# Normalising the last group's attention outputs token by token, and issuing the tail's regrouping transfers from two engines

## The reference

```python
x = x + _L0_conv_ref(_gn(x), w_qkv, w_o)      # attention: 12 heads of 16, 1024 tokens
x = x + _L1_conv_ref(_gn(x), w1, b1, w2, b2, bias_w, bias_b)
# _L0: attn = softmax(q k^T * 16 ** -0.5);  out = (attn @ v) @ w_o
# _L1: rfftn over the 32 x 32 positions, two block matmuls (4 blocks of 48) with
#      bias and relu on the complex spectrum, irfftn; plus x @ bias_w.T + bias_b
```

## Time and profile before

| | |
|---|---|
| median of 3 runs | 1517.59 us (1516.69 to 1521.7) |
| profiled execution, its time | 1528.75 us |
| profiled execution, its span | 1527.0 us |
| TensorE, busy | 1445.3 us (95%) |
| VectorE, busy | 1158.3 us (76%) |
| ScalarE, busy | 1009.0 us (66%) |
| GpSimd, busy | 187.6 us (12%) |
| queue q1 (all of the kernel's transfers) | 100992 packets, 105.44 MB, 30.1% of 16 engines' span |
| chain that ended last | PE 80%, DVE 6%, DMA 6%, SPq 2% |

### The profile page before, as it was taken

The page is one execution under the profiler, slowest core; times in us unless marked ns, Lnnn a source line. Parts: engine busy times, 40 slices in busy tenths (PEclk is TensorE's granted clock), DMA queues, the critical chain, the costliest instruction groups (busy, mean ns, idle before and its releaser), DMA issues.

```text
span 1527.0 us, 27399 instructions
## 1 busy us (share of the span) xinstructions
PE 1445.3 (95%) x9972; PEld 695.3 (46%) x9972; DVE 1158.3 (76%) x2153; ACT 1009.0 (66%) x2017; POOL 187.6 (12%) x277
## 2 busy tenths in 40 slices
PE   7699989999999999999999999999999999999787
PEld 4344333444545454444545444544544443434354
DVE  3695888888789878987789878997799878874131
ACT  1064777577767777677767777677767777668312
POOL 2000000140001300140011300040012100030000
PEclk7696999999999999999999999999999999999988
DMA  4430312213332414323422324333431333211313
GB/s 113 73 64 2 84 29 61 62 56 81 80 92 64 87 45 103 78 68 76 92 85 58 82 69 85 71 83 65 89 85 43 78 91 77 66 35 50 77 28 80
DMA packets 101126, 107.19 MB, mean 70 GB/s; under 512 B 25152, under 2 KB 77824, under 8 KB 100992
## 3 DMA queue, kind: packets, MB, share of 16 engines
q1 hardware_dynamic: 100992, 105.44, 30.1%
HBM read 27.51 MB, written 6.68 MB: 22 GB/s over the span
## 4 chain that ended last, share of the span: by engine, by line
PE 80%; DVE 6%; DMA 6%; SPq 2%; issue 2%; POOL 1%; ACT 1%; DVEq 0%; POOLq 0%; ACTq 0%
PE o_acc L1268 22%; PE ring L1247 15%; PE scores L1215 15%; PE ring L1291 10%; DVE row_max L1023 5%; DMA inv_all<-inv_rows 4%; PE ring L1280 3%; PE ring L1400 2%; PE ring L1393 2%; PE ring L1387 2%; SPq L663 2%; PE ring L1379 2%; PE scores L1291 1%; PE ring L1302 1%; PE ring L1406 1%
## 5 line engine op out<-in xcount | busy, mean ns | idle before, releaser
L1023 DVE TENSOR_REDUCE row_max<-ring 128x1 f32<-128x512 f32 x1536 | 975.2, 683 | 185.6 <-PE ring L1247 179.0
L931 ACT ACTIVATE probs<-scores 128x512 f32<-128x512 f32 x1536 | 829.0, 600 | 281.3 <-PE scores L1215 280.3
L1247 PE MATMUL ring<-k_stack,q_stack 48*128 48x512 f32 x1536 | 594.6, 469 | 26.7 <-DVE row_max L1023 24.3
L1215 PE MATMUL scores<-q_stack,k_stack 50*128 50x512 f32 x1536 | 598.7, 465 | 1.3 <-ACT probs L931 1.2
L1268 PE MATMUL o_acc<-probs,v_aug 128*18 128x512 f32 x3072 | 412.1, 609 | 2.4 <-ACT probs L931 1.2
L1215 PEld LDWEIGHTS scores<-q_stack,k_stack 50*128 50x128 f32 x1536 | 246.9, 188 | 319.6 <-ACT probs L931 294.9
L1247 PEld LDWEIGHTS ring<-k_stack,q_stack 48*128 48x128 f32 x1536 | 249.3, 191 | 145.4 <-DVE row_max L1023 97.3
L572 POOL TENSOR_TENSOR inv_all<-o_raw,inv_all 128x1024 f32<-128x1024 f32 x23 | 54.5, 2371 | 594.3 <-DMA inv_all<-inv_rows 594.3
L1268 PEld LDWEIGHTS o_acc<-probs,v_aug 128*18 128x18 f32 x3072 | 52.2, 96 | 124.5 <-issue 88.3
L1291 PE MATMUL ring<-xt,w_qk 64*128 64x256 f32 x504 | 62.3, 379 | 0.0
L1291 PE MATMUL ring<-wo,o_t 64*128 64x192 f32 x366 | 39.5, 346 | 16.1 <-DMA o_t<-inv_all 16.1
(11 more groups left out here) (152 smaller groups left out, 1112.6 us busy)
## 6 DMA issues: line engine op xcount, KB each, us to landing
q_stack<-qk_parts SPq DMA_DIRECT2D x288, 64.0 KB, 2.2
k_stack<-qk_parts SPq DMA_DIRECT2D x144, 128.0 KB, 4.3
inv_all<-inv_rows SPq DMA_DIRECT2D x24, 512.0 KB
rows_b<-rows_a SPq DMA_DIRECT2D x128, 96.0 KB, 2.8
spec_b<-spec_a SPq DMA_DIRECT2D x64, 102.0 KB, 2.3
x_in<-in_x_dram SPq DMA_DIRECT2D x8, 768.0 KB, 5.0
x_res<-in_x_dram SPq DMA_DIRECT2D x8, 768.0 KB, 4.7
o_t<-inv_all SPq DMA_DIRECT2D x192, 32.0 KB, 1.9
```

The costliest lines, as they stand in the source:

```text
L931: nc.scalar.activation(probs[:, GH * (s % 2) + h, :], scores[:, n % SCORE_BANKS, :], ACT.Exp, scale=SCALE).then_inc(probs_made, 1)
L1023: nc.vector.tensor_reduce(row_max[:, which, m:m + 1], max_bank(g, unit, i), AX.X, ALU.max).then_inc(max_taken, 1)
L1215: mm(scores[:, n % SCORE_BANKS, :], k_stack[rows, 2 * g + hp, P * kt:P * (kt + 1)], q_stack[rows, g, half, hp, :], start=True, stop=True). ...
L1247: mm(max_bank(g, unit, i), q_stack[rows, g, half, hp, P * qt:P * (qt + 1)], k_stack[rows, 2 * g + hp, HALF * which:HALF * (which + 1)], st ...
```

## The change

1. **The last group's outputs.** `sums_down`, `invert_sums`, `sums_back`, `spread_inverse`, `normalise_o` and `pack` are no longer done for the last slot of image 7. Instead TensorE transposes the 8 blocks of 128 tokens of `o_raw` into the banks `scores[:, 0]` and `scores[:, 1]`, right behind the last `pv` and ahead of the late pieces of image 6. VectorE, for each half, takes the reciprocal of the 16 sums of a token row and multiplies the outputs by it, into `o_tokens` (a view of `inv_all`), ahead of its late pieces. Behind the late pieces TensorE turns the 8 blocks back with 8 matmuls by the identity into `scores[:, 2]`, and ScalarE copies that bank to `o_t` with one instruction. `proj` of image 7 waits for this copy.
2. **The regrouping transfers of the tail.** They are shared by SP and ScalarE: of `regroup_rows` ScalarE issues the last piece's 2 of 8; of `stack_spectrum` one part each (2 and 2 for a chunk); of `regroup_mixed` one part each (3 and 3); of `regroup_lines` every other tile (4 and 4). ScalarE's stand in its program behind the copy that they need. The bodies of images 0 to 7 are left as they were. SP's store of image 6 is now its first transfer of the tail.
3. **`BUSY_LATE`:** "start" from 10 to 1, and 4 new ones behind `("lin", 7)`, which is the last `lin` pair, just ahead of `idftw`. "end" was read nowhere and is gone.

```diff
         BUSY = (2, 2, 1, 2, 2)
-        BUSY_LATE = {"start": 10, ("turn", 2): 1, ("mean", 0): 1, ("var", 0): 2, ("spread", 0): 2,
-                     ("dftw", 3): 3, ("dfth", 5): 2, ("mix2", 4): 6, "end": 2}
+        BUSY_LATE = {"start": 1, ("turn", 2): 1, ("mean", 0): 1, ("var", 0): 2, ("spread", 0): 2,
+                     ("dftw", 3): 3, ("dfth", 5): 2, ("mix2", 4): 6, ("lin", 7): 4}
...
             def tail():
-                b, slot = NB - 1, NG * NB - 1
-                sums_down(slot)
-                sums_back(slot)
-                spread_inverse(slot)
+                b = NB - 1
                 store(b - 1)
-                pack(b, NG - 1)
-                for k in range(4):
-                    regroup_rows(b, k)
-                stack_spectrum(b, 0)
-                stack_spectrum(b, 1)
-                regroup_mixed(b)
-                regroup_lines(b)
+                for k in range(3):
+                    regroup_rows(sp, b, k)
+                for chunk in range(2):
+                    stack_spectrum(sp, b, chunk, (0,))
+                regroup_mixed(sp, b, (0,))
+                regroup_lines(sp, b, range(0, NT, 2))
...
             def tail():
                 take_o(NG * NB - 1, 1)
                 late_pieces(post_piece)
+                act.wait_ge(o_turned_back, 1)
+                nc.scalar.copy(o_t[:, NG - 1, :], scores[:, 2, :]).then_inc(o_placed, 1)
+                b = NB - 1
                 for kind, k in POST:
-                    post_piece(NB - 1, kind, k, late_bank(kind, k))
+                    post_piece(b, kind, k, late_bank(kind, k))
+                    if (kind, k) == ("dftw", 3):
+                        regroup_rows(act, b, k)
+                    if kind == "dfth" and k % 3 == 2:
+                        stack_spectrum(act, b, k // 3, (1,))
+                    if (kind, k) == ("mix2", 4):
+                        regroup_mixed(act, b, (1,))
+                    if (kind, k) == ("idfth", 3):
+                        regroup_lines(act, b, range(1, NT, 2))
...
             def tail():
+                dve.wait_ge(o_packed, 16 * PACKS * (NG * NB - 1))
+                for half in range(2):
+                    dve.wait_ge(o_turned, half + 1)
+                    rows = scores[:, half, :].rearrange("p (t h d) -> p t h d", t=NT // 2, h=GH)
+                    inverse = sums[:, GH * NT // 2 * half:GH * NT // 2 * (half + 1)].rearrange(
+                        "p (t h) -> p t h", h=GH).unsqueeze(3)
+                    nc.vector.reciprocal(inverse, rows[:, :, :, HD:HD + 1]).then_inc(o_by_token, 1)
+                    dve.wait_ge(o_by_token, 2 * half + 1)
+                    nc.vector.tensor_tensor(o_tokens[:, NT // 2 * half:NT // 2 * (half + 1), :, :],
+                                            rows[:, :, :, 0:HD],
+                                            inverse.broadcast_to([P, NT // 2, GH, HD]),
+                                            ALU.mult).then_inc(o_by_token, 1)
                 late_pieces(post_piece)
-                invert_sums(NG * NB - 1)
-                normalise_o(dve, nc.vector, NG * NB - 1)
...
             def tail():
                 pv(NB - 1, NG - 1, STEPS - 1)
+                pe.wait_ge(probs_made, TILES * NG * NB)
+                for half in range(2):
+                    pe.wait_ge(o_out, 2 * (NG * NB - 1) + half + 1)
+                    for t in range(NT // 2):
+                        at = HALF * half + P * t
+                        last = nc.tensor.transpose(scores[:, half, P * t:P * (t + 1)],
+                                                   o_raw[:, at:at + P], ident)
+                    last.then_inc(o_turned, 1)
...
-                pe.wait_ge(probs_made, TILES * NG * NB)
-                pe.wait_ge(o_out, 2 * NG * NB)
+                pe.wait_ge(o_by_token, 4)
+                for t in range(NT // 2):
+                    for half in range(2):
+                        last = mm(scores[ROWS * half:ROWS * (half + 1), 2, P * t:P * (t + 1)],
+                                  o_tokens[:, t + NT // 2 * half, :, :].rearrange("p h d -> p (h d)"),
+                                  ident, start=True, stop=True)
+                last.then_inc(o_turned_back, 1)
                 keep_busy(BUSY_LATE["start"])
```

81 lines of the change are left out of this document (45 added, 36 removed).

## The result

| | before | changed |
|---|---|---|
| median of 4 runs each | 1519.64 us (1516.69 to 1523.37) | 1499.19 us (1496.07 to 1506.02) |
| ratio, with 95% interval | | 0.987 (0.9826 to 0.9915) |
| profiled execution, span | 1527.0 us | 1495.3 us |
| last `pv` to end of span | 99.77 us | 78.13 us |

The change made the kernel 20.4 us faster by the medians; the forecast was 23.3 us less, with 1494.3 us and a range of 1490.5 to 1502.5 us. Run again on another occasion, the changed kernel had a median of 1495.6 us against 1517.55 us, ratio 0.9857 (0.9834 to 0.988). By the time alone one could not tell the forecast from its rivals: 1499.19 us lies within the whole range, but above the forecast's own 1491.5 to 1496.5, and between rival B (1497.0) and rival A (1501.4). What decides is where the time went.

A forecast was written before the change was run, and what follows sets the result against it. After the last `pv`, a serial chain of transfers, then TensorE alternating with SP's transfers, and the clock bound the kernel. Terms 15.1 + 1.9 + 1.2 + 0.6 + 0 + 1.8 + 2.7 = 23.3 us: 1517.6 to 1494.3 us, range 1490.5 to 1502.5.

The forecast's parts named there:

- rival B: Ahead of `idftw`: issues overlap, but the clock falls all the same; price 2.7 us, giving 1497.0 us; chance 0.20.
- rival A: Shared transfers of the tail: the two engines' issues don't overlap, giving 1501.4 us; chance 0.23.
- The outputs' path: Last `pv` to `proj`: without the serial chain of transfers `proj` starts earlier, -15.1 us (bounds -13 to -15.7).
- `proj` at full clock: `proj` of image 7: all four pairs run at full clock, -1.9 us (bounds 0 to -2.1).
- `regroup_rows`: Wait before `dfth`: SP and ScalarE both finish issuing two issues earlier, -1.2 us (bounds 0 to -1.3).
- `stack_spectrum`: Wait before `mix1`: first chunk lands 1.28 us earlier, but fillers let only -0.6 us be used.
- `regroup_mixed`: Wait before `idfth`: three issues fewer free 1.9 us, but the chain stands on fillers, so 0 us.
- `regroup_lines`: Wait before `idftw`: eight issues in a row become four and four, -1.8 us (between 1.1 and 2.55).
- Fillers ahead of `idftw`: Wait for the lines: four fillers shorten TensorE's idleness; if the clock holds through `idftw`, -2.7 us.
- C: Shared transfers: an issue holds ScalarE until its transfer has landed, giving 1525.9 us, slower than before; chance 0.03.

## Why the prediction was right, and where it was off

**The outputs' path: right, term for term.** -15.15 us for -15.1. The transposes took 1.43 us for eight including the wait for the second half; the late pieces began 1.36 us later than before, counted from the last `pv`, where 1.5 was taken; VectorE's operations were 0.26 and 0.42 us against 0.3 and 0.42, and hidden. The chain of rows 3 was removed and nothing took its place. Run alone, this part gave 17.5 us of tail, with `proj`'s clock in it.

**`proj` at full clock: right,** -2.07 us for -1.9. With the ten fillers on the new path it was 5.02 us as well.

**`regroup_rows`: wrong.** The step "Both finish about 1.28 us (two issues) earlier", with the bounds 0 to -1.3, took the landing as the last issue plus a constant of 3.18 us. The constant was 4.81. The landing came 0.34 us later behind the copy, and the stage became 0.31 us longer, which is outside the bounds. Three experiments moved the last issue or the tiles, and the landing didn't follow; it stands 7.65 to 8.05 us behind the first issue. It is set by the flow of the eight transfers, and 0.4 us of that is the pairing of partitions; the rest is open. I had counted the load of the DMA engines for the lines and not for the rows, where the share was only 0.5 to 0.7 against the lines' 0.86; but a share below 1 didn't mean room.

**`stack_spectrum`: the number right by luck, the step wrong.** -0.57 us for -0.6. "The first chunk lands 1.28 us earlier by the issues" failed as the same step did for the rows: behind its last copy the chunk landed 4.02 us later in the kernel before and 3.64 us in the changed one, 0.4 us less, since the last transfer took 2.99 us instead of 2.14. The other 0.2 us came from the clock, which fell a little later within `dfth` than in the kernel before. The fillers' end, which the forecast took as the limit, was a dead heat with the landing. With the same shared transfers the stage took 7.58 us in the second run of the changed kernel and 7.97 and 8.02 in two experiments, against 7.89 before, so this execution's agreement is no confirmation. The clock fell in `dfth` all the same, at 0.53 to 0.62 in the two stretches from 1456 to 1460 us of the changed kernel; the wait before it had not shrunk (2.45 us of idleness, 2.10 before).

**`regroup_mixed`: right,** -0.06 us for 0, but not with the reserve that the forecast saw. In the kernel before the last mixed row landed at 1507.38, 0.14 us ahead of the first `idfth`: the landing and the fillers ended together. Sharing gained 0.19 us there, not 1.9.

**`regroup_lines`: the mechanism right, the size off by 0.4 us:** -1.41 for -1.8. It lies within its bounds. The lower bound of 1.1 does not come out of the figures beside it, though (5 us less 4.3 is 0.7), and the load is no fixed amount of work: added up over the table of stretches, the lines' packets held the sixteen engines for 4.3 us before and 3.2 us in the changed kernel, and the rows' for 3.0 and 4.3 us. The issues grew from 0.64 to 0.70 us and the last landing from 2.70 to 3.51 us.

**Fillers ahead of `idftw`: right,** -2.69 us for -2.7, and 2.63 when taken out. Rival B (the clock falls all the same) didn't happen in any of the ten profiles that had these fillers and the short wait. TensorE idled 1.61 us there, where 1.3 was forecast.

**The rivals.** A (issues don't overlap) and C (an issue holds ScalarE until the landing) are both refuted by the two runs of four issues within 2.86 us. Some mutual delay exists: issues of 0.87 us among those of 0.61 and 0.66 in the lines, and two of 1.14 and 0.97 us at the small transfers of `regroup_mixed`, where SP alone took 0.62. So if the lock of rival A is shared, these runs show it held for a small part of an issue only.

**The sum.** -21.6 us of tail for -23.3; the rows miss 1.5 us and the lines 0.4, and small gains elsewhere give 0.2 back. 19.9 of the 21.6 us are three terms whose mechanism was right: the outputs' path, `proj` at full clock and the fillers. The shared transfers were a small part of the sum, and that is why a step that failed in three of their four places did the total little harm. The medians gave -20.4 and, on the other occasion, -21.9 us.

## What to carry to other kernels

Look for a serial chain of transfers that only changes where data lies, and ask what the idle compute engines would charge for the same: here two turns, two small multiplies and a copy (4.5 us together, 1.4 of them under other work) replaced 19 us. Fillers belong to the wait they cover; when the wait goes, count them again, because the same nine cost 0 before and 7.7 us after. And when issues are spread over two engines, expect only what the transfers behind them leave room for: of eight transfers in a row, the part saved was 1.4 of 2.55 us in one place and less than nothing in another. Last, when a stage comes out as forecast, look whether it does so in a second execution, and what its chain stands on there.

## What I had not expected of the hardware

- Two engines' transfers in flight together moved 114 to 121 GB/s at a DMA share of 1.0 to 1.2, and one engine's 133 to 179 GB/s at 0.5 to 0.7, both near the end of the rows, with the same packets into 16 partitions a transfer.
- With equal bytes and issues, the pairing of partitions alone was worth 0.85 us in the lines and 0.38 us in the rows.
- The landing of the last rows comes 1.1 to 1.3 us after their last packet, that of the lines 0.3 us. No run tells why.
- The same program up to the group norm had its clock fall there in eight of fourteen profiles for 3 to 4 us, in one for 10 us, and in five not at all. The short fall cost some 0.6 us of the stage, and the long one 2.3 us more, 0.6 of which are the rows' wait. What decides it is open.
- The body of the program, untouched, ended anywhere between 1413 and 1427 us; a change of 2 us in the tail can be seen in stage lengths and not in times.
